# Where the FFN bias is rounded and where batch 0's residual sum stands, in a cross-attention and FFN kernel

## The reference, cut to what matters

```python
# x: (16, 128, 512), context: (16, 128, 256), 16 heads of 32
x = x + xattn(layernorm(x), context)     # two softmax segments: 112 main keys, 16 "dca" keys
                                         # the result goes through Wo and gets the bias bo
x = x + ffn(layernorm(x), kernel, bias)

def fake_quant(t, axis):                 # 8 bits
    scale = max(abs(t), axis) / 127
    return clip(round(t / scale), -127, 127) * scale

def ffn(x, kernel, bias):
    y = fake_quant(x, -1) @ fake_quant(kernel, 0) + fake_quant(bias, -1)
    return fake_quant(relu(y), -1)
```

## Time and profile before

| | |
|---|---|
| Median of 3 runs | 354.7 us (354.21 to 355.06) |
| The profiled execution's own time | 354.8 us |
| Its span, first to last instruction | 353.0 us |
| PE busy | 321.9 us (91%) |
| DVE busy | 315.7 us (89%) |
| ACT busy | 221.9 us (63%) |
| POOL busy | 173.8 us (49%) |
| Mean granted TensorE clock | 0.991 of 2.4 GHz |

### The profile page before, as it was taken

One profiled execution on the slowest core, in us unless ns is written; L12 is line 12 of the kernel. 1 busy time (PEld: TensorE's weight loads), 2 busy tenths in 40 slices (PEclk: granted clock), 3 DMA queues, 4 the chain that ended last, 5 costly groups with the idle time before them and its releaser, 6 DMA issues.

```text
span 353.0 us, 7629 instructions
## 1 busy us (share of the span) xinstructions
PE 321.9 (91%) x2375; PEld 254.4 (72%) x2375; DVE 315.7 (89%) x804; ACT 221.9 (63%) x444; POOL 173.8 (49%) x261
## 2 busy tenths in 40 slices
PE   5799989998999999999999999999999999987871
PEld 1355658776788888887878887878787878775630
DVE  3999899998889999999999999999999999986665
ACT  3577886375576767676768585858585856572401
POOL 5211712264373828282828282828383837272720
PEclk9999999999899999999999999999999999999998
DMA  7880345132151514251515151424233313130002
GB/s 268 255 302 3 120 134 185 46 122 78 46 151 46 174 41 153 67 170 49 172 43 178 49 169 58 153 74 147 81 130 97 122 63 121 64 130 22 26 6 89
DMA packets 36451, 38.88 MB, mean 110 GB/s; under 512 B 8760, under 2 KB 27452, under 8 KB 36412
## 3 DMA queue, kind: packets, MB, share of 16 engines
q1 hardware_dynamic: 36044, 38.14, 33.2%
q10 hardware_dynamic: 368, 0.27, 0.3%
HBM read 16.89 MB, written 4.72 MB: 61 GB/s over the span
## 4 chain that ended last, share of the span: by engine, by line
PE 59%; POOL 8%; DVE 7%; issue 5%; ACT 2%; DMA 1%; POOLq 0%; DVEq 0%; ACTq 0%
PE bank L1334 33%; PE bank L1457 9%; POOL finals L536 5%; PE bank L1437 3%; PE bank L1438 3%; PE bank L1629 2%; PE bank L1426 2%; PE bank L1511 2%; PE bank L1516 1%; PE bank L1478 1%; POOL x_small L593 1%; DVE seg_out L1079 1%; PE bank L1619 1%; DVE rden L1073 1%; ACT prob_store L757 1%
## 5 line engine op out<-in xcount | busy, mean ns | idle before, releaser
L517 POOL TENSOR_TENSOR k_lo<-wkv_raw,k_hi 128x448 f16<-128x448 f32 x16 | 16.8, 1049 | 109.4 <-issue 101.5
L1457 PE MATMUL bank<-v_aug,prob_store 128*128 128x66 f32 x512 | 67.1, 274 | 2.1 <-ACT prob_store L757 2.1
L1457 PEld LDWEIGHTS bank<-v_aug,prob_store 128*128 128x128 f32 x512 | 63.1, 191 | 4.5 <-ACT prob_store L757 3.2
L768 ACT ACTIVATE wkv_raw<-bank,affine 128x448 f32<-128x448 f32 (+1 forms) x32 | 22.3, 748 | 40.7 <-PE bank L1511 40.7
L1066 DVE TENSOR_REDUCE neg_max<-bank 128x4 f32<-128x448 f32 (+1 forms) x128 | 44.9, 412 | 0.3 <-PE bank L1426 0.3
L757 ACT ACTIVATE prob_store<-bank,exp_scale 128x512 f32<-128x512 f32 x64 | 41.7, 678 | 4.9 <-PE bank L1438 4.8
L536 POOL TENSOR_TENSOR finals<-seg_out 128x128 f32<-128x128 f32 x64 | 34.5, 548 | 12.6 <-DVE seg_out L1079 12.2
L1437 PE MATMUL bank<-q_stack,k_stack 128*128 128x128 f16 x256 | 33.9, 220 | 0.6 <-ACT maxT L612 0.6
L1438 PE MATMUL bank<-maxT,sel 128*128 128x128 bf16 x256 | 33.7, 219 | 0.0
L1079 DVE TENSOR_TENSOR seg_out<-bank,rden 128x256 f32<-128x256 f32 x64 | 27.2, 425 | 4.0 <-POOL finals L536 1.7
L1437 PEld LDWEIGHTS bank<-q_stack,k_stack 128*128 128x128 f16 x256 | 26.4, 104 | 5.2 <-issue 3.9
(11 more groups left out here) (213 smaller groups left out, 886.2 us busy)
## 6 DMA issues: line engine op xcount, KB each, us to landing
x_in<-in_x SPq DMA_DIRECT2D x16, 256.0 KB, 3.0
q_stack<-q_hi SPq DMA_DIRECT2D x32, 128.0 KB, 2.1
q_stack<-q_lo SPq DMA_DIRECT2D x32, 128.0 KB, 2.1
k_stack<-k_hi SPq DMA_DIRECT2D x32, 128.0 KB, 2.1
k_stack<-k_lo SPq DMA_DIRECT2D x32, 128.0 KB, 2.1
out<-finals SPq DMA_DIRECT2D x16, 256.0 KB, 2.0
y_dcaT<-in_x SPq DMA_DIRECT2D x8, 256.0 KB, 2.8
x_res<-in_x SPq DMA_DIRECT2D x8, 256.0 KB, 2.8
```

The costliest lines, as they stand in the source:

```text
L768: s.activation(n.rearrange("p (c n) -> p c n", n=P)[:, :, 0:keys], src, ACT.Identity, bias=shift, scale=gain).then_inc(n_ready.sem, 1)
L1457: last = mm(bank[6 + gr % 2][:, VW * h:VW * (h + 1)], probs[:, gr % 2, h], v_aug[:, Bt.parity, HG * gr + h], start=True, stop=True)
```

## The change

The two passes over the FFN bias go from VectorE to GpSimd, in step 1 behind the dca columns and in front of k's low part. Its magnitude, scale and reciprocal stay on VectorE and move from the end of step 1 (in front of `maxima(0)`) to the place in front of q's low part; a new semaphore tells GpSimd when the reciprocal is there. And GpSimd's sum of x and output bias of batch 0 moves in step 0 from in front of `combine(0)` to behind `combine(3)`; for all other batches it stays.

```diff
@@ GpSimd
+            def setup_ffn_bias():
+
+                pool.wait_ge(fbstat_ready.sem, 1)
+                g.tensor_scalar(fb_row[:], fb_row[:], fb_stat[:, 2:3], ROUND, ALU.mult, ALU.add).then_inc(fbrnd_ready.sem, 1)
+                pool.wait_ge(fbrnd_ready.sem, 1)
+                g.tensor_scalar(fb_row[:], fb_row[:], ROUND, fb_stat[:, 1:2], ALU.subtract, ALU.mult
+                                ).then_inc(fbias_ready.sem, 1)
...
                         dca_columns(k_hi, kdca_hi)
                         dca_columns(k_lo, kdca_lo)
+                        if C is not None and C.first():
+                            setup_ffn_bias()
                         low(k_lo, k_n, k_hi, kn_ready, khi_ready, kstack_in, klo_ready, MAIN)
...
-                if Bt is not None:
+                def residual():
                     if Bt.first():
                         pool.wait_ge(out_bias_ready.sem, 1)
                     pool.wait_ge(*xres_loaded.of(Bt))
                     if Bt.has(1):
                         pool.wait_ge(*x1_ready.of(Bt.back(1)))
                     g.tensor_tensor(x_plus, x_res[Bt.parity], out_bias[:], ALU.add).then_inc(xplus_ready.sem, 1)
+
+                if Bt is not None and not Bt.first():
+                    residual()
                 if Bt is not None:
                     combine(0)
...
                 if Bt is not None:
                     combine(2)
                     combine(3)
+                    if Bt.first():
+                        residual()
@@ VectorE
             def setup_ffn_bias():
 
                 dve.wait_ge(fb_in.sem, 16)
                 link(v.tensor_reduce(fb_stat[:, 0:1], fb_row[:], AX.X, ALU.max, apply_absolute_value=True))
                 link(v.tensor_scalar(fb_stat[:, 1:2], fb_stat[:, 0:1], TINY, 1.0 / QMAX, ALU.max, ALU.mult))
-                link(v.reciprocal(fb_stat[:, 2:3], fb_stat[:, 1:2]))
-                link(v.tensor_scalar(fb_row[:], fb_row[:], fb_stat[:, 2:3], ROUND, ALU.mult, ALU.add))
-                v.tensor_scalar(fb_row[:], fb_row[:], ROUND, fb_stat[:, 1:2], ALU.subtract, ALU.mult
-                                ).then_inc(fbias_ready.sem, 1)
+                v.reciprocal(fb_stat[:, 2:3], fb_stat[:, 1:2]).then_inc(fbstat_ready.sem, 1)
...
+                if C is not None and C.first():
+                    setup_ffn_bias()
                 if N is not None and not N.second():
                     low_query()
                 if C is not None and C.first():
...
-                    if C is not None and C.first():
-                        setup_ffn_bias()
                     maxima(0)
                     maxima(1)
```

More of the change, by code:

```diff
@@ L222, in xattn_ffn @@
         fkscale_ready, fkint_ready, fbias_ready = signal("fkscale_ready"), signal("fkint_ready"), signal("fbias_ready")
-        pow2_ready = signal("pow2_ready")
+        pow2_ready, fbstat_ready, fbrnd_ready = signal("pow2_ready"), signal("fbstat_ready"), signal("fbrnd_ready")
         xres_loaded = parity_signal("xres_loaded")
```

## The result

The changed kernel takes 360.27 us (median of 4 runs, 358.12 to 363.72) against 354.88. The forecast was 355.3, with a range up to 356.4. By the ratio the change costs 4.8 us, and even the lower end of the interval, 2.8 us, is far above the 0.7 us that a measurement tells apart. The profiled execution took 359.43 us (span 357.6), 4.6 more than that of before. Lines of the new kernel are up to 15 higher than before: L1273 is the old L1259, L1042 the old L1030, L1469 the old L1457, L1490 the old L1478.

The account below looks back on a forecast made before the run. The bound was a chain of waits, nearly all on TensorE, leaving it for VectorE's bias between steps 1 and 2. -1.0 - 2.05 + 3.6 + 1.56 - 1.56 = +0.55 us on 354.8 gave 355.35 (355.3 against the median), range 353.6 to 356.4.

Parts of the forecast that it names:

- Part 1: Step 0: GpSimd's sum of batch 0 behind the combines lets VectorE and so TensorE come earlier, -1.0 us.
- Part 2: End of step 1: five bias instructions leave VectorE, so step 2's projection starts sooner after the transposes, -2.05 us.
- the old fall: Projection of step 2: the granted clock's fall after scattered TensorE idle time goes away, -1.56 us.
- Parts 3 and 4: Step 1: statistics before q's low part and passes queued on GpSimd delay L1259 and so TensorE, +3.6 us.
- The upper bound: Step 1, L1259's delay: each pass takes the longest L508's 1.29 us and is held besides, +4.8 us.
- The clock: Behind the new 4.1 us TensorE stall in step 1: granted clock falls, +1.56 us, bounds 0 and 3.1.
- Rival A: Behind the new 4.1 us stall: 1.2 GHz lasts through more stretches, up to +1.56 us more, 356.5; chance 0.17.
- B: Behind the new stall in step 1: the clock doesn't fall, or hardly, 353.7 us; chance 0.14.
- C: Step 1: GpSimd isn't held by VectorE, chain +2.0 instead of +3.6 us, 353.7 us; chance 0.13.
- D: Step 0: another wait replaces TensorE's removed one at 60.36, so the sum's move gains nothing, 356.3 us; chance 0.06.

Follow-up runs that it names:

- Before, kept busy in step 2: The kernel before, with ten unread identity products on TensorE in step 2, in front of the scores of groups 2 and 3; 354.02 us against 354.76, ratio 0.9987.
- TensorE kept busy: The changed kernel, with 24 unread identity products on TensorE in front of the third round of weighing of step 1; 354.89 us, 1.003 of before.
- the adding form: The changed kernel, with GpSimd's second pass adding the constant -ROUND instead of subtracting ROUND; 359.02 us (2 runs) against 359.43.
- the second profile: Profile of the changed kernel with both forms of the passes also done once early, in step -2, on 128 columns; 360.05 us (4 runs) against 359.43.
- passes in step 2: The changed kernel, with GpSimd's two passes moved to step 2 behind VectorE's low part of y, statistics still before q's low part; 352.92 us, 0.9971 of before.

## Why the prediction was wrong

- **Part 1 (-1.0): right.** Step 0 is 0.97 us shorter, and the sum's new place is hidden.
- **Part 2 with the old fall (-2.05 - 1.56 = -3.61): right in the sum.** Step 2 is 3.62 us shorter. "Before, kept busy in step 2" divides this into 1.40 for the clock and 2.22 for the wait, so each term was off by 0.16 us or so, in opposite directions, and an agreement to 0.01 us is luck.
- **Parts 3 and 4 (+3.6): the mechanism right, the term too small.** The queue on GpSimd held VectorE and so TensorE, as forecast, but with TensorE kept busy it measured +5.08. The step that failed is "L508 is the same form (one scalar per partition, one constant), 0.69 us alone". The kind of operands was taken for the form; a subtraction takes 2.0 us. That is 1.31 of the missing 1.48 us: with the adding form TensorE waits 4.21 us, where the forecast had 4.1. The upper bound, "If each pass takes the 1.29 us of the longest L508 and is held besides, +4.8", took a held instruction for a slow one and so didn't reach it either. The rest, 0.2 us, is put down to the order, which no run takes apart: the forecast gave the first pass its turn behind q's low part, while L1042 went first. The page "SBUF — State Buffer" of the Trainium skill says in "Who interferes with whom" that issue order decides who blocks; here the pass is recorded from 72.91 and L1042 from 73.36, and L1042 went ahead. The measurement decides.
- **The clock (+1.56): the term that failed most.** It measured 3.75 us (3.04 by the second profile). The step that failed is "take the same price, +1.56": it was taken from the one fall of before, which followed scattered waits of 1.5 us and lay in a run of full work, some 3.5 us of it. Here 1.2 GHz lasted for 8.48 us of work behind the wait. Why it lasted longer no run shows. Rival A named this, and was given a chance of 0.17 and at most 1.56 us more; it was +2.19 (+1.48 by the second profile). The forecast's bound for the whole price was 3.1. With every other term right, 2.19 us more would have been outside the range by itself.
- **The sum**, with the measured terms: -0.97 - 3.62 + 5.08 + 3.75 = +4.24, and 4.6 in the profiled executions' own times. The remaining 0.4 lies behind the last x transposes (67.11 us against 66.73 before), within the scatter of that stretch; steps 3 to 12 together take the same within 0.03 us.
- B, C and D are refuted: the clock fell, GpSimd was held, part 1 paid. The move of q's low part by the statistics is within the 0.90 us of step 1 that "passes in step 2" shows. That k's low part leaves later on SP's queue was taken to cost nothing; no run tests it alone.

## What to carry to other kernels

Before moving an instruction to an engine, ask first who is queued behind it there and who waits for those: the same 2.7 us of passes cost 27.36 - 19.46 = 7.9 us of step 1 in front of k's low part, the clock included, and next to nothing in an idle stretch a step later. Price an instruction by a row with the same operation, not only the same operands, and take a row's longest duration apart into held and own time. A new wait of several us on TensorE has to be priced with its clock, and slack is to be read only where the granted clock is full.

## What the runs showed of the hardware that was not expected

GpSimd's `tensor_scalar` with a subtraction in front takes 2.0 us for 512 columns, against 0.69 to 0.77 us for the forms that add (0.996 us for the same instruction with the constant's sign turned, beside VectorE's L1043 and so probably held at its start). A GpSimd instruction lost its turn to a VectorE instruction that is recorded after it (2.14 and 2.25 us for 0.69 us of work). And in one wait of 5.51 us TensorE's granted clock fell to 1.2 GHz for 10.23 us, which cost 3.0 to 3.75 us of time; where TensorE had products to do that nobody reads, it didn't fall.
